# Keys loaded in two column ranges, and probability tiles loaded from ScalarE's queue, in a three-part transformer layer

## What is computed

```python
# macaron: half a mixed low-rank FFN, attention, half an FFN
x = x + 0.5 * ffn(layernorm(x))
x = x + attn(layernorm(x))
x = x + 0.5 * ffn(layernorm(x))

def attn(x):                       # one head of width 2048
    z = layernorm(x) * gamma + beta
    q, k, v = z @ Wq, z @ Wk, z @ Wv          # three [2048, 2048] weights
    scores = (q @ k.T) / sqrt(2048)           # causal mask
    out = softmax(scores) @ v
    return out @ o_proj + x

def ffn(x):                        # K = 8 experts of rank R = 64
    h = relu(x @ W1 + b1)
    alpha = softmax(h @ W2 + b2)
    return sum_k alpha[k] * U[k] @ (V[k] @ x)
```

## Time and profile before

| what | value |
|---|---|
| median of 3 runs | 7833.34 us (7827.17 to 8227.19) |
| the profiled execution | 7839.64 us |
| its span (slowest core, core 2) | 7838.1 us |
| spans of the 8 cores | 7810.9 to 7838.1 us |
| mean granted TensorE clock | 0.876 to 0.879 of full speed |
| PE busy | 5995.2 us (76%) |
| POOL, DVE, ACT busy | 2210.5 us (28%), 1187.4 us (15%), 594.6 us (8%) |

### The profile page before, as it was taken

One profiled execution on the slowest core, in us unless ns is written; L12 is line 12 of the kernel. 1 busy time (PEld: TensorE's weight loads), 2 busy tenths in 40 slices (PEclk: granted clock), 3 DMA queues, 4 the chain that ended last, 5 costly groups with the idle time before them and its releaser, 6 DMA issues. The chain is left out here.

```text
span 7838.1 us, 92017 instructions; the slowest of 8 cores (7810.9 to 7838.1 us)
## 1 busy us (share of the span) xinstructions
PE 5995.2 (76%) x28887; PEld 2968.2 (38%) x29364; DVE 1187.4 (15%) x1270; ACT 594.6 (8%) x780; POOL 2210.5 (28%) x5708
## 2 busy tenths in 40 slices
PE   2799599536569998999992775367689974996898
PEld 2343343212224444444441333246534433433443
DVE  2211311331210011000010111000020013113112
ACT  1000100121110000000000000000010001000000
POOL 0350152013335555555551000121100001530450
PEclk7899799767779999999996887588889986998999
DMA  2112211311212222222223211311132222113113
GB/s 70 52 48 73 90 48 39 123 70 64 70 62 72 68 68 69 73 73 72 66 68 117 61 36 29 118 35 40 49 131 75 74 76 66 48 36 133 42 45 97
DMA packets 626192, 537.25 MB, mean 69 GB/s; under 512 B 226714, under 2 KB 572874, under 8 KB 602162
## 3 DMA queue, kind: packets, MB, share of 16 engines
q1 hardware_dynamic: 589362, 387.65, 17.1%
q0 software_dynamic: 36352, 143.69, 5.2%
HBM read 387.28 MB, written 143.82 MB: 68 GB/s over the span
## 5 line engine op out<-in xcount | busy, mean ns | idle before, releaser
L282 POOL CAST w1hi<-w1f 128x128 bf16<-128x128 f32 x2560 | 791.8, 309 | 1621.3 <-PE psA L456 577.3
L284 POOL TENSOR_TENSOR w1lo<-w1f,w1hi 128x128 bf16<-128x128 f32 x2560 | 1096.6, 428 | 379.0 <-POOL w1hi L282 11.3
L709 PE MATMUL psA<-bigA_hi,w1hi 128*128 128x512 bf16 x1997 | 608.9, 385 | 206.0 <-POOL w1lo L284 151.3
L456 PE MATMUL psA<-bigA_hi,w1hi 128*128 128x512 bf16 x1988 | 599.5, 381 | 28.3 <-DVE bigA_lo L416 19.8
L709 PE MATMUL psA<-bigA_hi,w1lo 128*128 128x512 bf16 x2021 | 611.2, 383 | 1.4
L456 PE MATMUL psA<-bigA_hi,w1lo 128*128 128x512 bf16 x2040 | 610.6, 381 | 0.4
L709 PE MATMUL psA<-bigA_lo,w1hi 128*128 128x512 bf16 x2001 | 608.4, 384 | 2.5
L456 PE MATMUL psA<-bigA_lo,w1hi 128*128 128x512 bf16 x1988 | 599.5, 381 | 3.2
L935 PE MATMUL psA<-sv_hi,bigA_hi 128*128 128x256 bf16 x1152 | 170.9, 300 | 278.0 <-DVE ht_lo L294 166.5
L709 PEld LDWEIGHTS psA<-bigA_hi,w1hi 128*128 128x128 bf16 x2048 | 197.3, 99 | 456.6 <-issue 237.2
L294 DVE TENSOR_TENSOR ht_lo<-psA,ht_hi 128x256 bf16<-128x256 f32 (+1 forms) x192 | 132.7, 691 | 1544.5 <-DMA aot_lo<-ht_lo 552.0
(11 more groups left out here) (185 smaller groups left out, 6213.1 us busy)
## 6 DMA issues: line engine op xcount, KB each, us to landing
w1f<-qkv SPq DMA_DIRECT2D x1536, 64.0 KB, 1.8
w1f<-W SPq DMA_DIRECT2D x1024, 64.0 KB, 1.9
xa<-x_scratch SPq DMA_DIRECT2D x32, 1024.0 KB, 4.8
xa<-x SPq DMA_DIRECT2D x16, 1024.0 KB, 4.9
x_scratch<-xa POOLq DMA_DIRECT2D x16, 1024.0 KB, 8.4
xp_scratch<-xa POOLq DMA_DIRECT2D x16, 1024.0 KB, 4.2
xa<-xp_scratch SPq DMA_DIRECT2D x16, 1024.0 KB, 5.3
out<-xa POOLq DMA_DIRECT2D x16, 1024.0 KB, 8.7
```

Source lines behind the costliest of these rows:

```text
L282: p.do("gpsimd", lambda e: e.tensor_copy(out=hi_ap, in_=src_ap), reads=src_bufs, writes=[hi_buf], inc="g")
L284: p.do("gpsimd", lambda e: e.tensor_tensor(out=lo_ap, in0=src_ap, in1=hi_ap, op=ALU.subtract), reads=list(src_bufs) + [hi_buf], writes=[lo ...
L456: last = e.matmul(out=pa[:, n0:n1], lhsT=wop[:, ws * 128:(ws + 1) * 128], rhs=yop[:, di * TG + n0:di * TG + n1], start=(di == 0 and pi == ...
L709: last = e.matmul(out=pa[:, n0 - th * THW:n1 - th * THW], lhsT=wop[:, ws * 128:(ws + 1) * 128], rhs=zop[:, di * S + n0:di * S + n1], start ...
```

## The change

The two loops that load K become four kinds of loads under two new names. Columns 0 to 511 of each key chunk (keys 0 to 511) go under K_early, hi and lo in turn, 32 loads of 128 KB; columns 512 to 2047 go under K_late, hi and lo in turn, 32 loads of 384 KB. The score matmuls read K_early, and K_late only where a segment reaches past key 512, which begins with tile 4. A new helper dma_in_hw issues a load from ACT, and load_pt uses it for all PT loads. The rest stands as before.

```diff
+    def dma_in_hw(dst_ap, src_ap, writes, reads=()):
+        sem = "lhB_" + writes[0].name
+        return p.do("scalar", lambda e, d=dst_ap, s=src_ap: e.dma_start(out=d, in_=s),
+                    reads=reads, writes=writes, inc=sem, n=16)
...
-        Kh, Kl = gb("bigA_hi"), gb("bigA_lo")
+        KT0 = min(512, S)
+        Kearly, Klate = gb("K_early"), gb("K_late")
         for dc in range(NC):
-            dma_in(bigA_hi[:, dc * S:(dc + 1) * S], k_hi_h[dc * 128:(dc + 1) * 128, :],
-                   writes=[Kh], reads=[gb("k_h")])
-        for dc in range(NC):
-            dma_in(bigA_lo[:, dc * S:(dc + 1) * S], k_lo_h[dc * 128:(dc + 1) * 128, :],
-                   writes=[Kl], reads=[gb("k_h")])
+            dma_in(bigA_hi[:, dc * S:dc * S + KT0], k_hi_h[dc * 128:(dc + 1) * 128, 0:KT0],
+                   writes=[Kearly], reads=[gb("k_h")])
+            dma_in(bigA_lo[:, dc * S:dc * S + KT0], k_lo_h[dc * 128:(dc + 1) * 128, 0:KT0],
+                   writes=[Kearly], reads=[gb("k_h")])
+        if S > KT0:
+            for dc in range(NC):
+                dma_in(bigA_hi[:, dc * S + KT0:(dc + 1) * S], k_hi_h[dc * 128:(dc + 1) * 128, KT0:],
+                       writes=[Klate], reads=[gb("k_h")])
+                dma_in(bigA_lo[:, dc * S + KT0:(dc + 1) * S], k_lo_h[dc * 128:(dc + 1) * 128, KT0:],
+                       writes=[Klate], reads=[gb("k_h")])
...
-                p.do("tensor", mm_sc1, reads=[qh, Kh], writes=pab, inc="t")
-                p.do("tensor", mm_sc23, reads=[qh, ql, Kh, Kl], writes=pab, inc="t")
+                kreads = [Kearly] + ([Klate] if s1 > KT0 else [])
+                p.do("tensor", mm_sc1, reads=[qh] + kreads, writes=pab, inc="t")
+                p.do("tensor", mm_sc23, reads=[qh, ql] + kreads, writes=pab, inc="t")
...
-                dma_in(sv_hi[:, s_ * QG:(s_ + 1) * QG],
+                dma_in_hw(sv_hi[:, s_ * QG:(s_ + 1) * QG],
...
-                dma_in(sv_lo[:, s_ * QG:(s_ + 1) * QG],
+                dma_in_hw(sv_lo[:, s_ * QG:(s_ + 1) * QG],
```

More of the change, by code:

```diff
@@ L908, in load_pt @@
                 slot_of[(g, kc)] = s_
-                dma_in(sv_hi[:, s_ * QG:(s_ + 1) * QG],
-                       pt_hi_h[kc * 128:(kc + 1) * 128, g * QG:(g + 1) * QG],
-                       writes=[slot_buf[s_]], reads=[gb("pt_h")])
-                dma_in(sv_lo[:, s_ * QG:(s_ + 1) * QG],
-                       pt_lo_h[kc * 128:(kc + 1) * 128, g * QG:(g + 1) * QG],
-                       writes=[slot_buf[s_]], reads=[gb("pt_h")])
+                dma_in_hw(sv_hi[:, s_ * QG:(s_ + 1) * QG],
+                          pt_hi_h[kc * 128:(kc + 1) * 128, g * QG:(g + 1) * QG],
+                          writes=[slot_buf[s_]], reads=[gb("pt_h")])
+                dma_in_hw(sv_lo[:, s_ * QG:(s_ + 1) * QG],
+                          pt_lo_h[kc * 128:(kc + 1) * 128, g * QG:(g + 1) * QG],
+                          writes=[slot_buf[s_]], reads=[gb("pt_h")])
         load_pt(0)
```

## The result

The changed kernel is slower: the ratio of its times to those of the kernel before is 1.0229 (95% interval 1.0214 to 1.0245), which is 179 us on 7833.8. Its runs in the ratio gave 8006.7 to 8019.1 us, beside 7827.2 to 7834.7 of the kernel before. Executions in which the cores of a die ran at a lower clock are left out, since with them the medians of ten runs each, 8016.2 and 8214.0 us, can't be compared; where such a die left an experiment without an interval, the spans of the other die's four cores are given.

What follows compares the result with a forecast made beforehand. It took chained K load latencies, with q behind them, to bound the head, and ht_hi's store waits to pace attention x V. 60 - 7 + 136 - 8 - 6 = +175 us gave 8008 us on the 7833.3 median, range 7975 to 8048.

Steps and rivals of the forecast that it cites:

- K in 64 loads in turn: Head of the scores: twice as many K loads, each waiting for the one before to land, +60 us (bounds +33 to +74).
- start of V (first load to V lo): Start of attention x V: V's loads no longer stand behind four PT loads, so V lo's first matmuls come earlier, -7 us.
- the seven seams: Between query groups in attention x V: PT loads cannot start before ACT's last activation of the group before, +136 us (+118 to +174).
- first steps shorter, less contention: Attention x V: a group's first step is one store, not two (-8 us), and loads no longer run beside steps (-6).
- The line between the 64 KB and the 512 KB load: K loads at the head: interpolating 2.05 and 3.29 us prices 128 KB at 2.23 and 384 KB at 2.94 us.
- rival D: Start of attention x V: V's stream holds up group 0's PT loads, 15.9 us each, total about 8038 us; chance 0.07.
- the contention's -6: Attention x V: some 20 steps no longer run beside loads, 0.3 us each, -6 us (bounds 0 and -12).
- A (cost by bytes): K loads and seams: loads in turn cost only their bytes, total 7832 us, weak form about 7980; chance 0.08.
- B (early start): Head of the scores: TensorE starts while the late K half still loads, 30 us earlier than now, total 7918; chance 0.02.
- C (dearer from ACT): PT loads: issuing from ACT costs 0.3 us more on each of 140 issues, +42, about 8050 us; chance 0.09.

Runs made afterwards that it cites:

- e7: Kernel before with K split, each K load under its own name, and tile 0's q loads between early and late parts: ratio 0.9945 to before.
- e4: Kernel before with only the four PT loads of group 0 issued from ACT: one run of 7835.4 us, beside 7836.5 of the kernel before.
- e3: Kernel before, PT loads still on SP but held until ACT's last block of the group before: four cores spanned 7943.2 to 7955.5 us.
- e1: Changed kernel with the PT loads put back on SP, so only K is split: 7909.4 us in one execution, beside 7836.5 of the kernel before.
- e10: Repeat of the K split alone, PT loads on SP, for an interval: ratio 1.008 (1.005 to 1.0109) to the kernel before.
- e6: Kernel before with the 32 K loads under 32 names, nothing split: four cores spanned 7759.9 to 7781.2 us, beside 7832.6 to 7842.3 before.
- e2: Kernel before with only the PT loads moved to ACT, K loaded as before: lowest runs 7954.1 and 7957.2 us, no interval.
- e5: Changed kernel with two names per PT slot, so no PT load waits for another: ratio 1.0113 (1.0089 to 1.0138) to the kernel before.

## Why the prediction was right, and which step of it was off

The forecast was 8008 us and 2.2% slower; the ratio 1.0229 on 7833.8 is 8013, and single runs gave 8007 to 8019. Direction, size and both mechanisms hold. The sum has five terms, the last two taken together here:

| term | forecast | slowest cores (after 0, before 2) | means of eight cores |
|---|---|---|---|
| K in 64 loads in turn | +60 | +63.4 | +61.8 |
| start of V (first load to V lo) | -7 | -6.3 | -3.5 |
| the seven seams | +136 | +133.5 | +133.7 |
| first steps shorter, less contention | -14 | -5.6 | -13.1 |
| sum | +175 | +185 | +179 |

The spans of the two slowest cores differ by 173.6 us and the means by 173.9. The rest is in stretches that the change does not touch, such as the start to the first K load, which vary from core to core.

*The step that was off* is the term for the start, put at -7. It was 7.7 us for V's earlier issue less 0.7 for the PT bytes beside V, and both parts were mis-sized. The 7.7 was read from one core: over the eight cores of the kernel before V's first load stood 4.6 to 8.4 us behind the first PT load, mean 6.2. And V took 2.7 us longer beside the PT loads (33.3 against 30.6 from its first load to V lo), not 0.7. That leaves -3.5 in place of -7. The errors of the other three (+1.8, -2.3 and +0.9) are smaller, and they partly cancel: that the sum is within 5 us of the ratio is in part luck.

*K.* The line between the 64 KB and the 512 KB load put 2.23 and 2.94 us on 128 and 384 KB; it was 2.32 and 2.95. The early half was mis-sized by 0.09 us a load, 3 us in all, and lies a little over the upper bound drawn from q's loads (2.25). Nothing started early, since q stood behind all of K: the first score matmul is put down to q and comes 10.6 us behind q's first load. In e7, where q's loads stand ahead of the late half and no K load waits for another, the first matmul came at 26.4 us.

*Start.* The term's mechanism holds, though not its size: four PT loads beside V's stream took 23.2 us and not 21, and were covered by V lo. The rival D (15.9 us each) is out by the changed kernel's own rows and by e4. The Trainium skill's page "DMA: Bandwidth & Descriptors" (section "Issuing engines are not separate DMA queues") says that DMAs issued by different engines run on the same 16 DMA engines and interleave. This trace agrees: V took the 2.7 us longer, and the PT loads took 5 to 10 us each. That the move to another queue gives nothing by itself at the seams agrees with e3, where queue and place were told apart.

*Seams.* Forecast 14.5, 20.6, 26.8, 33.0, 38.8, 44.2, 50.0; measured 14.9, 21.3, 26.5, 32.7, 37.0, 43.4, 49.2, the sum 227.9 against 225.0. One detail was wrong: ACT's queue issues the first load 0.02 to 0.07 us after its activation starts, not 0.45 after.

*Given back.* The sum holds, its parts only roughly. The first steps after seams 1 to 4 went from 4.79, 4.79, 6.39 and 4.90 us to 3.03, 3.01, 3.02 and 4.45 (means of eight cores): 7.4 us given back and not 8. Where an ordinary step of 4.8 stood, the gain is 1.8 and not 2.4; the 6.39 at seam 3 was longer for a reason that isn't known (on core 2 SP's last PT load was issued 5 us ahead of it). The other 5.7 us of the 13.1 answer to the contention's -6. The whole term shows in the other kernels too: the steps of the eight groups sum to 621.0 to 624.6 us where SP loads PT ahead (before, e1, e10, e4, e6, e7) and to 608.1 to 610.1 where the loads stand behind the group (changed, e2, e3, e5). No run tells its two parts from each other. In the pair of slowest cores alone only 5.6 us of it are seen, in part since core 2 of the kernel before had a short group 0 (81.7 us against a mean of 85.1).

The rivals. A (cost by bytes) fell with the K spacings, with e1's ratio and with e5. B (early start) did not happen, and e7 adds that an early first tile is worth nothing while the second one's q is late. C (dearer from ACT) fell: issues from ACT in turn took 0.33 to 0.46 us and once 0.68, and e3 on SP costs the same. D fell as said.

## What to carry to other kernels

Count landings, not bytes: where the loads of a stream wait for one another, most of each is not its bytes (here 2.05 us for 64 KB, 2.32 for 128, 2.95 for 384 and 3.29 for 512), and cutting them smaller makes the stream longer. Splitting a load so that work can start early does nothing while another input of that work stands behind the whole stream in the same queue; move that input too, and look at the next tile's as well. A queue that has nothing else to do is the place for prefetches; put behind the last result of a stage they cannot start before it, whatever engine issues them. And read small terms from all cores: the start term looked like 6 us on one pair of cores and was 4.

## What was not expected

- A load behind an activation in ACT's queue is issued while the activation still runs: 5058.85 against 5058.83, and 5683.66 against 5683.59, with activations of 0.38 us.
- Loads that wait for nothing go out of ACT's queue every 0.485 us, and the time from the last issue to the next activation was then longer, 11.2 us against 9.7 with the loads in turn.
- Starting TensorE 34 us earlier than in e6 (26.4 against 60.9 us after the first K load) gained nothing: tile 1 came 8 us later than in e6, its first matmul put down to q.
